# Value projections moved into the first attention units, the score stack read in quarters, max splits on GpSimd

## The reference

```python
x = x + L0_xattn(layernorm(x), ctx, ctx, mask)    # 16 heads of 8, q from x, k and v from the context, softmax, @ Wo.T + bo
x = x + L0_ffn(layernorm(x))                      # 8 experts 128 -> 512 -> 128, relu, router keeps the top 2
x = x + L1_xattn(layernorm(x), ctx)               # 16 heads of 64; layer norms of latents and of the context,
                                                  # k, v = split(ln(ctx) @ Wkv); rope on k; scores clipped to +-11; softmax; @ Wo + bo
x = x + L1_ffn(layernorm(x))                      # input rounded to int8 steps, ternary weights, scale, bias
```

## Time and profile before

| | us |
|---|---|
| runs | 277.05, 278.46 (median), 306.36 |
| profiled execution | 277.17 |
| its span, first to last instruction | 275.3 |
| PE, DVE, ACT, POOL busy | 246.5, 185.9, 124.7, 44.5 |
| mean granted TensorE clock | 0.983 |

### The profile page before, as it was taken

One profiled execution on the slowest core, in us unless ns is written; L12 is line 12 of the kernel. 1 busy time (PEld: TensorE's weight loads), 2 busy tenths in 40 slices (PEclk: granted clock), 3 DMA queues, 4 the chain that ended last, 5 costly groups with the idle time before them and its releaser, 6 DMA issues.

```text
span 275.3 us, 5245 instructions
## 1 busy us (share of the span) xinstructions
PE 246.5 (90%) x2064; PEld 159.4 (58%) x2064; DVE 185.9 (68%) x420; ACT 124.7 (45%) x189; POOL 44.5 (16%) x58
## 2 busy tenths in 40 slices
PE   0769897999977989999999999999999999999952
PEld 0544334344433548788897787886666668666541
DVE  7740798999986432547566962077996975799554
ACT  5277347667655655423434234554436341544100
POOL 7518000000000100241333633001200000110011
PEclk9979999999999999999999999999999999999995
DMA  7557485468310000006015062600000000000001
GB/s 213 170 144 140 151 175 129 89 257 306 88 67 0 2 4 0 0 2 152 0 33 124 0 154 61 169 2 0 2 2 0 2 2 0 2 1 2 2 0 39
DMA packets 7688, 18.52 MB, mean 67 GB/s; under 512 B 1144, under 2 KB 3520, under 8 KB 7120
## 3 DMA queue, kind: packets, MB, share of 16 engines
q1 hardware_dynamic: 7005, 12.90, 19.0%
q10 hardware_dynamic: 659, 5.29, 5.5%
HBM read 12.45 MB, written 1.45 MB: 50 GB/s over the span
## 4 chain that ended last, share of the span: by engine, by line
PE 73%; DVE 15%; ACT 4%; issue 3%; DMA 2%; SPq 0%; POOL 0%; DVEq 0%; ACTq 0%
PE b L893 43%; PE st L893 27%; DVE nmax L694 5%; DVE reg_p L832 2%; DMA ctxT<-in_ctxT 2%; DVE rs L844 2%; ACT reg_p L560 1%; ACT reg_p L606 1%; PE b L897 1%; PE b L1006 1%; ACT ctx_tok L514 1%; SPq L325 0%; DVE reg_q L708 0%; DVE w L839 0%; DVE y L635 0%
## 5 line engine op out<-in xcount | busy, mean ns | idle before, releaser
L893 PE MATMUL b<-reg_p,v 128*32 128x256 f32 (+1 forms) x768 | 50.7, 382 | 1.4 <-ACT reg_z L571 1.1
L694 DVE TENSOR_REDUCE nmax<-b 128x1 f32<-128x512 f32 x64 | 42.2, 686 | 13.1 <-PE b L893 12.0
L606 ACT ACTIVATE reg_p<-st 128x1024 f32<-128x1024 f32 x32 | 31.0, 1022 | 43.5 <-PE st L893 43.5
L583 ACT ACTIVATE reg_z<-st,small 128x256 f32<-128x256 f32 x56 | 24.5, 473 | 32.8 <-PE st L893 32.8
L560 ACT ACTIVATE reg_p<-st 128x1024 f32<-128x1024 f32 x32 | 32.3, 1020 | 15.5 <-PE st L893 14.7
L431 POOL TENSOR_TENSOR rstd<-ve,mhalf 128x2 f32<-128x2 f32 (+2 forms) x10 | 8.7, 871 | 161.6 <-DVE ve L629 159.1
L893 PEld LDWEIGHTS b<-w,reg_z 128*128 128x128 f32 x256 | 30.9, 192 | 4.9 <-issue 4.5
L893 PEld LDWEIGHTS b<-reg_p,v 128*32 128x32 f32 (+1 forms) x768 | 19.8, 102 | 22.9 <-issue 11.1
L893 PE MATMUL st<-v,reg_k 64*128 64x256 f32 x256 | 32.0, 389 | 0.3 <-ACT reg_p L606 0.2
L893 PE MATMUL b<-w,reg_z 128*128 128x128 f32 x256 | 31.5, 276 | 0.0
L832 DVE TENSOR_SCALAR reg_p<-reg_p 128x1024 f32<-128x1024 f32 x32 | 22.5, 703 | 10.9 <-ACT reg_p L606 10.7
(11 more groups left out here) (168 smaller groups left out, 291.3 us busy)
## 6 DMA issues: line engine op xcount, KB each, us to landing
w<-in_w ACTq DMA_DIRECT2D x2, 2048.0 KB, 7.8
reg_k<-reg_p SPq DMA_DIRECT2D x16, 128.0 KB, 2.3
reg_k<-reg_q SPq DMA_DIRECT2D x16, 128.0 KB, 2.3
reg_k<-k_scr SPq DMA_DIRECT2D x6, 192.0 KB
reg_k<-k_scr SPq DMA_DIRECT2D x3, 384.0 KB
k_scr<-reg_z SPq DMA_DIRECT2D x6, 128.0 KB
reg_q<-q_scr SPq DMA_DIRECT2D x6, 96.0 KB
reg_q<-q_scr SPq DMA_DIRECT2D x3, 192.0 KB
```

The costliest lines, as they stand in the source:

```text
L583: nc.scalar.activation(hT[:, n % 2, f, :], hidden(n, f), ACT.Relu, bias=b1[:, n % E, f:f + 1]).then_inc(h_sb, 1)
L606: nc.scalar.activation(prob[:, u % RING1, :], st2[u % 2][:, :], ACT.Exp, scale=DK1 ** -0.5).then_inc(st_exp, 1)
L694: nc.vector.tensor_reduce(nmax[:, q, i:i + 1], bank[4 + mx % 2], AX.X, ALU.max, negate=True).then_inc(mx_done, 1)
L893: return nc.tensor.matmul(o, l, r, start=start, stop=stop)
```

## The change

- The first 7 value projections stand ahead of `order`, 6 come with two maxima each (12 maxima instead of 16 ahead of unit 0), and the last three stand in units 0, 1 and 2, through bank 6, each behind ACT's eviction of the one before. Unit 0 waits for 13. The memset of bank 6 becomes an item "pz" behind unit 4.
- SP: the mask's scratch write, the wait for it and the mask rows go ahead of the key parts. The stack of batch 0 is read in quarters of four heads, queries first, each with a semaphore of its own, and not in halves; so there are 24 reads where there were 12, all ahead of the scratch writes of batch 1.
- POOL makes the mask parts ahead of the context's pow. DVE makes `shift` ahead of the keys' product with the mask, not within their splits.
- PE's query projection of layer 0 stands ahead of the layer 0 values. ACT normalises the context in pairs of tiles between its evictions, evicts the query projection in two halves (batch 0's first, batch 1's behind the first `context`), and the keys of batch 1 and POOL's query splits wait for the second.
- ms of groups 1 to 7 goes from DVE to POOL; DVE keeps group 0. Both halves of mr are copied by ACT. An even unit now waits for the half that it needs, not every fourth for both.

```diff
-EARLY = 8
+EARLY = 7
+FRONT = 13
...
-        for n in range(EARLY, 2 * CT):
+        for n in range(EARLY, FRONT):
             next_maxima(2)
             order.append(("v1", n))
...
         for u in range(UNITS):
             order.append(("st", u))
+            if u < 2 * CT - FRONT:
+                order.append(("v1", FRONT + u))
+            if u == 4:
+                order.append(("pz",))
             next_maxima(1)
...
+            sp.wait_ge(mparts, 1)
+            sp.dma_start(m_scr.rearrange("j (p n) -> p j n", p=16), mpart[:, :, :]).then_inc(scr_m, 16)
+            sp.wait_ge(scr_m, 16)
+            for c in range(B):
+                sp.dma_start(Ks[MASK_ROW:MASK_ROW + NPART, c, :, :],
+                             m_scr[:, None, c * S2:(c + 1) * S2].broadcast_to([NPART, H, S2])).then_inc(mask_rows, 16)
             for j in range(NPART):
                 sp.wait_ge(parts, j + 1)
                 sp.dma_start(k_scr[0, :, j], kparts[:, j, :]).then_inc(scr_k[0], 16)
...
-            for i in range(NPART):
-                read_k(0, i, halves[0], stack[0][0])
             sp.wait_ge(scr_q[0], 16)
...
+            for n in range(G):
+                for i in range(NPART):
+                    read_q(0, i, quarters[n], stack[0][n])
+                for i in range(NPART):
+                    read_k(0, i, quarters[n], stack[0][n])
...
             power(TT)
-            power(CT, 0)
             pool.wait_ge(in_mask, 16)
...
+            power(CT, 0)
...
-            pool.wait_ge(q0_f, 1)
+            pool.wait_ge(q0_f, 2)
...
+                if kind == "ms" and item[1]:
+
+                    q = item[1]
+                    pool.wait_ge(mx_split, q)
+                    pool.wait_ge(mx_done, (q + 1) * 4 * QT)
+                    link(nc.gpsimd.tensor_copy(maxpart[:, q, 0, :], nmax[:, q, :]))
+                    link(nc.gpsimd.tensor_tensor(maxres[:, :], nmax[:, q, :], maxpart[:, q, 0, :], ALU.subtract))
+                    link(nc.gpsimd.tensor_copy(maxpart[:, q, 1, :], maxres[:, :]))
+                    nc.gpsimd.tensor_tensor(maxpart[:, q, 2, :], maxres[:, :], maxpart[:, q, 1, :],
+                                            ALU.subtract).then_inc(mx_split, 1)
+                    pool.wait_ge(mx_split, q + 1)
+                elif kind == "wo":
                     power(QT)
...
+            act.wait_ge(ctx_shift, 1)
+            normalise(0, 2)
             act.wait_ge(tr, 1)
             nc.scalar.activation(yT[:, :], bank[7], ACT.Copy).then_inc(yT_sb, 1)
+            normalise(2, 4)
             act.wait_ge(q0_ps, 1)
-            nc.scalar.activation(qf, bank[6], ACT.Copy, scale=1.0 / math.sqrt(DK0)).then_inc(q0_f, 1)
-            act.wait_ge(ctx_shift, 1)
-            normalise(0)
+            nc.scalar.activation(qf[:, 0:S], bank[6][:, 0:S], ACT.Copy, scale=1.0 / math.sqrt(DK0)).then_inc(q0_f, 1)
+            normalise(4, 6)
             values0(0)
-            normalise(1)
             act.wait_ge(in_small, 16 * 2)
             context(0)
+            normalise(6, 8)
+            nc.scalar.activation(qf[:, S:2 * S], bank[6][:, S:2 * S], ACT.Copy, scale=1.0 / math.sqrt(DK0)).then_inc(q0_f, 1)
             values0(1)
             context(1)
...
-                elif kind == "mr" and item[2] == 0:
-                    b, h0 = item[1] // G, 4 * (item[1] % G)
+                elif kind == "mr":
+                    b, h0 = item[1] // G, 4 * (item[1] % G) + 2 * item[2]
                     act.wait_ge(misc_ps, misc[item])
...
             dve.wait_ge(k0_ps, 2)
+            dve.wait_ge(q0_f, 2)
             nc.vector.tensor_tensor(kf[:, S2:2 * S2], bank[5], maskb[:, S2:2 * S2], ALU.mult).then_inc(kf_sb, 1)
-            nc.vector.memset(bank[6], 0.0).then_inc(o0_sb, 1)
...
-                elif kind == "ms":
-                    q = item[1]
+                elif kind == "ms" and item[1] == 0:
...
-                elif kind == "mr" and item[2] == 1:
-                    b, h0 = item[1] // G, 4 * (item[1] % G) + 2
-                    take(item)
-                    nc.vector.tensor_copy(Qs[MAX_ROW:BLOCK, b, h0:h0 + 2, :].rearrange("j h q -> j (h q)"),
-                                          bank[7][0:NPART, :]).then_inc(misc_done, 1)
+                elif kind == "pz":
+
+                    dve.wait_ge(v1_sb, 2 * CT)
+                    nc.vector.memset(bank[6], 0.0).then_inc(o0_sb, 1)
...
-            values0(0)
             pe.wait_ge(yT_sb, 1)
             mm(bank[6], l0w[:, 0, :], yT[:, :]).then_inc(q0_ps, 1)
+            values0(0)
             context(0)
...
-                    if u % 4 == 0:
-                        pe.wait_ge(misc_done, misc[("mr", u // 4, 1)])
+                    if u % 2 == 0:
+                        pe.wait_ge(misc_done, misc[("mr", u // 4, u % 4 // 2)])
                     if u == 0:
-                        pe.wait_ge(v1_sb, 2 * CT)
+                        pe.wait_ge(v1_sb, FRONT)
```

More of the change, by code:

```diff
@@ L186, in build @@
         scr_m, mask_rows = sem("scr_m"), sem("mask_rows")
-        stack = [[sem("stack0_0"), sem("stack0_1")], [sem("stack1")]]
+        stack = [[sem(f"stack0_{n}") for n in range(G)], [sem("stack1")]]
         ctx_shift, ctx_normed = sem("ctx_shift"), sem("ctx_normed")
@@ L345, in read_q @@
                              .broadcast_to([DK0, NPART, n * S])).then_inc(s, 16)
-            halves = [slice(n * H // 2, (n + 1) * H // 2) for n in range(2)]
+            quarters = [slice(4 * n, 4 * n + 4) for n in range(G)]
             whole = slice(0, H)
+            sp.wait_ge(mparts, 1)
[4 more added lines that the diff above has]
+                             m_scr[:, None, c * S2:(c + 1) * S2].broadcast_to([NPART, H, S2])).then_inc(mask_rows, 16)
             for j in range(NPART):
@@ L508, in values, with normalise @@
                 act.wait_ge(v1_ps, n + 1)
-                nc.scalar.activation(v1[:, n // 2, 512 * (n % 2):512 * (n % 2) + 512], bank[n % 4],
+                nc.scalar.activation(v1[:, n // 2, 512 * (n % 2):512 * (n % 2) + 512], bank[6 if n >= FRONT else n % 4],
                                      ACT.Copy).then_inc(v1_sb, 1)
-            def normalise(i):
-                for c in range(4 * i, 4 * i + 4):
+            def normalise(first, end):
+                for c in range(first, end):
                     last = nc.scalar.activation(ctx_tok[:, c, :], ctx_tok[:, c, :], ACT.Identity, scale=rstd[:, c:c + 1],
@@ L666, in _ @@
             norms[0] += 1
+            dve.wait_ge(pow_done, 2)
+            nc.vector.scalar_tensor_tensor(out=shift[:, :], in0=mv[:, 0:CT, 0], scalar=-1.0, in1=rstd[:, 0:CT],
+                                           op0=ALU.mult, op1=ALU.mult).then_inc(ctx_shift, 1)
             dve.wait_ge(in_maskb, 16)
@@ L672, in _ @@
             link(nc.vector.tensor_tensor(res, kf[:, 0:S2], kparts[:, 0, :], ALU.subtract))
-            dve.wait_ge(pow_done, 2)
-            nc.vector.scalar_tensor_tensor(out=shift[:, :], in0=mv[:, 0:CT, 0], scalar=-1.0, in1=rstd[:, 0:CT],
-                                           op0=ALU.mult, op1=ALU.mult).then_inc(ctx_shift, 1)
             part(nc.vector.tensor_copy(kparts[:, 1, :], res))
@@ L901, in values @@
                 pe.wait_ge(ctxn, 2 if n >= CT else 1)
-                if n >= 4:
+                if n > FRONT:
+                    pe.wait_ge(v1_sb, n)
+                elif n == FRONT:
+                    pe.wait_ge(q0_f, 2)
+                elif n >= 4:
                     pe.wait_ge(v1_sb, n - 3)
@@ L905, in values @@
                     pe.wait_ge(v0_sb, n - 1)
-                mm(bank[n % 4], ctxT[:, (n // 2) * P:(n // 2 + 1) * P],
+                mm(bank[6 if n >= FRONT else n % 4], ctxT[:, (n // 2) * P:(n // 2 + 1) * P],
                    wv1[:, 512 * (n % 2):512 * (n % 2) + 512]).then_inc(v1_ps, 1)
@@ L926, in context @@
             def context(i):
[L927 removed]
+                pe.wait_ge(ctx_normed, 2 * i + 2)
                 transposes(ctx_tok, 4 * i, 4, bank[7 * i]).then_inc(tr, 1)
[L930 removed]
             pe.wait_ge(yT_sb, 1)
             mm(bank[6], l0w[:, 0, :], yT[:, :]).then_inc(q0_ps, 1)
+            values0(0)
             context(0)
@@ L960, in _ @@
                     if i == 0 and q < G:
-                        pe.wait_ge(stack[0][q // 2], 16 * 2 * NPART)
+                        pe.wait_ge(stack[0][q], 16 * 2 * NPART)
                     elif i == 0:
```

24 lines of the change are left out of this document (5 added, 19 removed).

## The result

The changed kernel takes 278.45 us (median of 20 executions, 276.74 to 286.16) beside 278.15 for the kernel before (20 executions, 274.58 to 306.88); the ratio is 1.0061, 95% interval [1.0037, 1.0086]. So the change costs some 1.7 us where a gain of 1.3 was forecast. The profiled execution of after took 279.04 us with a span of 277.3 (before 277.17 and 275.3).

A forecast was written before the change was run, and what follows sets the result against it. DVE was taken to pace the attention stage, PE close behind. From 277.17 us, -4.3 (first matmul), -1.3 (to unit 8), -1.0 (groups), +2.8 (stall), -1.7, +3.4 (tail), +0.8 (clock) gave -1.3: 275.9, range 270.8 to 279.6.

The forecast's parts named there:

- first score matmul: Front, layer 0: PE reaches it at 24.2 instead of 28.57, without waiting for transfers, a gain of 4.3 us.
- from there to unit 8: First units: unit 0 at 35.0, unit 8 at 50.0 instead of 55.63, a further gain of 1.3 us.
- three groups: Units 8 to 20: 6.85 us per four units instead of 7.18, a gain of 1.0 us.
- stall on the stack: ACT's first o0 eviction waits for batch 1's stack, landing at 54.2 beside the w1 load: costs 2.8 us.
- units 20 to 24: Attention tail: first two tail items meet no max rows in bank 7; 8.55 us instead of 10.24, gaining 1.7.
- It starts there: Front: the query projection starts when yT is ready near 12.1, not at 12.96, a gain of 0.85 us.
- rival D: Front: first quarter lands no sooner than 28, as 24 DMAs are issue bound; 277.5 us, chance 0.07.
- P + 5.63 = 6.85: Steady four units: P, last reduction's end to max-row matmuls, is 1.2 on POOL; 6.85 us against 7.18.
- Rival C: Group splits: POOL's steps take twice DVE's, 0.34 each, four units 7.45; 278.5 us, chance 0.10.
- Rival B: Batch 1's stack decides: with w1 at an even split it lands near 57.5, giving 279.2 us; chance 0.13.
- Which stood at 24.91. They land near 35.1: SP's queue: batch 1's key writes slip behind the quarters to 30.8, so its stack starts 0.8 us later.
- Tail, 3.4 + 0.8: Behind unit 24: the last two maxima wait on DVE behind wo, costing 3.4 us; half clock after PE's pause, 0.8.

The follow-up runs named there:

- g1: Changed kernel with wo behind unit 25 and the first layer 0 values ahead of the query projection: 273.06 us, ratio 0.9842.
- f4: Changed front with the units, splits, copies and bank 6 memset place of the kernel before, all 16 value projections ahead: 297.26 us, ratio 1.0076.
- f2: Changed kernel with wo behind unit 25, max rows one score matmul later, first half copied by DVE, second by ACT: 274.20 us, ratio 0.9884.
- g2: Changed kernel with wo behind unit 25, all splits on DVE and max rows one score matmul later: 273.92 us, ratio 0.9869.
- e2: Changed kernel with the splits of all groups back on DVE, copies staying on ACT: 283.76 us, ratio 1.0008.
- e4: Changed kernel with both max-row items one score matmul later: 277.06 us, ratio 0.9969.
- f1: Changed kernel with wo behind unit 25 and all splits on DVE: 279.24 us, ratio 0.9847.
- h2: g1 with the w1 load issued at unit 9 instead of unit 6: 273.39 us, ratio 0.9872.
- e1: Changed kernel with the item wo one unit later, behind unit 25 and the last two maxima: 274.34 us, ratio 0.9895.
- g4: Front of the kernel before (halves, keys first, mask rows in the middle) with the changed kernel's units: 280.93 us, ratio 1.014.
- f3: f1 with the stack of batch 0 read in halves, queries first, 12 reads instead of 24: 278.58 us, ratio 1.0046.
- e3: Changed front with the units, splits and copies of the kernel before, all 16 value projections ahead, bank 6 memset at unit 4: 294.13 us, ratio 1.0078.
- g3: Changed kernel with all value projections and 16 maxima ahead of unit 0: 292.50 us, no ratio.
- h3: g1 with first quarter's keys issued before SP's wait for query parts, plus f2's later max rows and copies on DVE and ACT: 271.30 us, ratio 0.9799.

## Why the prediction was wrong

The range held the time (278.45 in 270.8 to 279.6) and a time within 2% of before's was its likeliest verdict and is the measured one; the sign was wrong. The step that failed is the length of a group of four units; that the sum lands this near is luck, since the stall that was forecast didn't come either. Set against the spans, the forecast was 274.0 and the profile 277.3. The 3.3 us come apart like this:

| step | forecast, us | profile, us | off |
|---|---|---|---|
| first score matmul | 24.2 | 25.75 | +1.55 |
| from there to unit 8 | 25.8 | 26.7 | +0.9 |
| three groups | 20.55 | 22.8 | +2.3 |
| stall on the stack | 2.8 | 0 | -2.8 |
| units 20 to 24 | 8.55 | 8.85 | +0.3 |
| unit 24 to the last values products, with half clock | 17.2 | 18.4 | +1.2 |
| from there to the end | 174.9 | 174.8 | -0.1 |

- **Front, +1.55.** "It starts there", and the sum 13.0 + 1.71 + 0.44 and so on behind it, took over durations from a PE that had work before. The query projection now comes behind 1.90 us of idling and takes 2.07; the transposes and the key projection were 1.1 longer too, and the eight small matmuls behind them 0.8 shorter. g1 shows the first of it. But much of the 1.55 differs between executions: in the ten profiled ones with this order of the front and quarters the first score matmul starts anywhere from 24.21 (f4), the forecast's own value, to 26.22 (f2, g2). The forecast was right that PE doesn't wait for a transfer there, and rival D falls.
- **Groups, "P + 5.63 = 6.85": the step that failed.** The forecast named the loop (POOL's split, PE, DVE) but let nearly all of PE's items between the reductions pass behind DVE's work. Term by term, in the group from 49.67 to 57.28: max rows, unit and score matmul up to the first reduction 1.18 (forecast 1.07); the next two reductions 1.57 (1.34), since the second waits for PE; the gap 0.81 (0.58), again a wait for PE; the last four reductions 2.75 (2.64), with one more wait for PE; P 1.30 (1.2). Followed as a chain, PE holds 4.8 us of the group (0.38 + 0.54 + 1.84 + 0.54 + 0.23 + 1.27), two reductions 1.4 and POOL's hand-off 1.30. In sum a group is 0.75 over the forecast and 0.42 over before, where a gain of 0.33 was claimed; some 0.65 of the 0.75 is DVE behind PE's items, 0.1 POOL. e2 and e4 fit the loop: to shorten either of its two ends, POOL's or the rows', shortens it by 0.34 and 0.43.
- **Rival C** named the loss on GpSimd but for a wrong reason. The Trainium skill, GPSIMD Engine Reference, Engine selection, has such work at about twice VectorE's time; at 8 columns a step took 0.20 beside 0.18, and what was lost is the hand-off between engines on both sides. The prediction says that the rows at 64 and 256 columns show the factor of two; they hold no VectorE row of 64 columns, and at 256 they have 0.67 beside VectorE's 0.42, on other operands. That the rival's 278.5 is the measured time is chance: its 0.34 a step didn't come.
- **Stall, 2.8: it didn't come.** The forecast has ACT ready for the eviction at 50.4 and the stack at 54.2, 52.5 without w1. The units were 2.4 us later than forecast at unit 8, and the eviction ran at 52.70 and waited for nothing, so the stack had landed by then: with slower units there was little left to wait for. With shorter groups ACT did wait, 2.25 us in e2, 2.40 in e4, 2.97 in f1. Whether w1 costs the stack the 1.7 us that the forecast gave it stays open: without w1 beside it the wait ended at 51.85 (h2), with it anywhere from 51.77 to 54.42 (g1, e1, e2, e4, f1), and h2 is no faster than g1. The Trainium skill, DMA: Bandwidth & Descriptors, Queues, rings and completion order, has the engines take turns between queues; read as an even split, which was the forecast's estimate, this would have landed the stack near 57, and no run here shows that. The big load did take longer, 10.4 us instead of 7.7 (8.0 in g4, where it goes out at 49.37 with the stack long read). Rival B falls: no wait for the stack ended behind 54.42. Two errors of opposite sign, in the groups and in the stall, nearly cancel.
- **Issue order.** "Which stood at 24.91. They land near 35.1" took SP's issue time as the price of the quarters. Those reads start at 36.85, and in f3, with half the count and the writes issued 7 us sooner, at 37.11 all the same.
- **Tail, 3.4 + 0.8.** Mechanism and size were right: pause 4.07 (forecast 4.6), ended by POOL, half clock behind it, 4.1 us given back by e1. It is only 1.2 short, half clock included, which had 0.8 and lasted from 90 to 96.
- **Not seen at all:** that the lead in the front can be lost to a half clock at 45 to 55, as in e3, f4 and g3, and that the work moved into the first units (three projections, four maxima) goes with its absence.

In all the change is three things: a front worth 1.3 to 2.5 us, units and groups that together bring about nothing, and a tail that costs 4.1.

## To carry to other kernels

When work is taken off the busiest engine, add up the whole loop that then closes (split, rows, units, score matmul, reduction) with the pitches of the trace, hand-offs included, and not the engine's own sum less the work taken off. When maxima or any feed of the pipeline are thinned out ahead of its start, look at what stands in front of the last of them at the end of the stage: one item moved by one unit was worth more here than any other edit. And a position that leaves PE idle can cost twice: in after the clock was halved in the pause of 4.07 us and for some 4.5 us behind it, and in ten of eleven profiled executions a slow projection followed the idling in the front.

## What the runs showed of the hardware

- A float32 128 x 512 projection of two records took 2.07 or 2.08 us behind 0.69 to 1.90 us of idling on TensorE in ten profiled executions and 1.12 in an eleventh (f4, behind 1.60), and 1.02 to 1.54 behind work; in after (2.07) and g1 (1.13) the granted clock reads 1.00 in the windows around it.
- TensorE busy 3.96 and 4.57 of 5 us (f4, g3) was followed by a granted clock of 0.50 (the 1.2 GHz level) for 10 us in one execution and over 60 us in the other; after, busy 4.10 of 5 in 45 to 50, and h3, busy 3.99 in 40 to 45, kept 1.00. The busy share alone doesn't tell them apart.
- In a pause of TensorE of 4.07 us (after, until 91.56) the granted clock fell to 0.50, and it read 0.50 until 96; with one of 1.15 us at the same place (e1) it stayed at 1.00.
- Two loaded DMA queues: a 2 MB load took 10.4 us (after) to 12.6 us (g1) beside many small reads, 7.7 (before) and 8.0 us (g4) without them. What the small reads pay is not told: 51.85 without the load, 51.77 to 54.42 with it.
- A step of 128 x 8 takes 0.20 us on GpSimd and 0.18 on VectorE; four chained steps with hand-off 1.30 and 0.95.
